# Attention loop in another order, and two unbinding products of the last block moved from GpSimd to VectorE

## What is computed

```python
def unit_projection(x):
    f = jnp.fft.fft(x)
    f = f / (jnp.abs(f) + EPS)
    return jnp.fft.ifft(f).real
...
        query = unit_projection(jnp.einsum('bsd,ed->bse', x, Wq) + bq)
        keys = unit_projection(jnp.einsum('bsd,ed->bse', x, Wk) + bk)
        values = unit_projection(jnp.einsum('bsd,ed->bse', x, Wv) + bv)
        x_k = bind(keys, values)          # ifft(fft(keys) * fft(values)).real
        s = jnp.cumsum(x_k, axis=1)
        out = unbind(s, query)            # ifft(fft(s) * conj(fft(query))).real
...
    h = _layernorm(x, axis=-1) * (1 + ca) + sa
    x = x + ga * _L0_attn_ref(h, ...)
    h = _layernorm(x, axis=-1) * (1 + cb) + sb
    x = x + gb * _L0_ffn_ref(h, ...)      # top 2 of 8 experts by h @ gate_w, softmax of the two, SwiGLU
```

## Time and profile before

| | |
|---|---|
| median of three runs | 638.22 us (636.01 to 638.6) |
| the profiled execution | 634.83 us |
| its span, first to last instruction | 633.0 us |
| TensorE busy | 565.5 us (89%) |
| VectorE busy | 490.1 us (77%) |
| ScalarE busy | 301.8 us (48%) |
| GpSimd busy | 322.2 us (51%) |
| mean granted TensorE clock | 0.935 |

### The profile page before, as it was taken

How to read it: one execution, slowest core, us unless ns; L and a number is a source line. 1 busy time by engine, 2 the same in 40 slices (tenths; PEclk the granted TensorE clock), 3 DMA queues, 4 the chain that set the end, 5 groups by cost and what they waited for, 6 DMA issues and landing times.

```text
span 633.0 us, 13199 instructions
## 1 busy us (share of the span) xinstructions
PE 565.5 (89%) x4005; PEld 428.1 (68%) x4006; DVE 490.1 (77%) x1058; ACT 301.8 (48%) x497; POOL 322.2 (51%) x213
## 2 busy tenths in 40 slices
PE   6888999899999966559699999999999999999982
PEld 5444554555546543326488888888888888888871
DVE  1238789989998988897378888888888888888881
ACT  3664877877786762532333333333333333333330
POOL 0002132441413243000638888888888888888554
PEclk9798999989997995857799999999999999999996
DMA  9213273652735328622747777777777777777632
GB/s 318 86 61 124 67 204 100 193 149 83 216 101 169 102 88 285 211 38 67 196 62 134 135 138 135 137 136 134 134 135 133 133 133 133 133 134 134 98 35 34
DMA packets 86942, 82.93 MB, mean 131 GB/s; under 512 B 48628, under 2 KB 76276, under 8 KB 86648
## 3 DMA queue, kind: packets, MB, share of 16 engines
q0 software_dynamic: 18480, 34.51, 30.3%
q1 hardware_dynamic: 67128, 47.07, 25.9%
q10 hardware_dynamic: 1296, 0.87, 0.4%
HBM read 45.90 MB, written 23.15 MB: 109 GB/s over the span
## 4 chain that ended last, share of the span: by engine, by line
PE 70%; DVE 12%; ACT 6%; issue 6%; DMA 3%; POOL 1%; POOLq 0%; SPq 0%; ACTq 0%; DVEq 0%
PE ps L703 33%; PE ps L720 16%; PE ps L484 9%; PE ps L540 3%; ACT region L801 2%; PE ps L494 2%; PE ps L636 1%; DMA w_stage<-in_w 1%; ACT region L857 1%; DVE region L1140 1%; DVE region L1180 1%; PE ps L425 1%; POOL region L1544 1%; PE ps L527 1%; DMA region<-in_dft 1%
## 5 line engine op out<-in xcount | busy, mean ns | idle before, releaser
L703 PE MATMUL ps<-region,w_sb 128*128 128x256 f16 x1872 | 213.4, 275 | 2.7 <-ACT region L939 2.7
L703 PEld LDWEIGHTS ps<-region,w_sb 128*128 x1872 | 184.2, 99 | 25.7 <-issue 3.0
L1574 POOL DMA_INDIRECT out_rows<-w_stage,region x78 | 150.5, 1930 | 48.5 <-DVE w_stage L1491 26.5
L1564 POOL DMA_INDIRECT region<-h_scratch,region x78 | 106.0, 1359 | 71.4 <-DVE region L1437 47.9
L1459 DVE TENSOR_SCALAR region<-ps,region 128x256 f32<-128x256 f32 x156 | 68.1, 478 | 61.0 <-PE ps L703 60.9
L720 PE MATMUL ps<-region 128*128 x936 | 110.2, 275 | 3.4 <-DVE region L1473 3.4
L720 PEld LDWEIGHTS ps<-region 128*128 128x128 f16 x936 | 92.3, 99 | 15.0 <-issue 3.6
L1015 ACT ACTIVATE region<-ps,region 128x256 f32<-128x256 f32 x156 | 65.5, 471 | 76.4 <-PE ps L703 76.4
L1025 ACT ACTIVATE region<-region 128x1024 f16<-128x1024 f32 x39 | 41.2, 1058 | 125.3 <-DVE region L1467 125.3
L484 PE MATMUL ps<-region 128*128 128x512 f32 x192 | 88.3, 617 | 8.4 <-ACT region L815 6.0
L1544 POOL TENSOR_TENSOR region<-region 128x512 f32<-128x512 f32 x32 | 39.7, 1267 | 94.3 <-DVE region L1167 94.3
(11 more groups left out here) (208 smaller groups left out, 683.8 us busy)
## 6 DMA issues: line engine op xcount, KB each, us to landing
w_stage<-in_w SPq DMA_DIRECT2D x20, 512.0 KB, 3.6
region<-in_x SPq DMA_DIRECT2D x8, 512.0 KB, 8.2
out_rows<-region SPq DMA_DIRECT2D x8, 512.0 KB, 3.0
h_scratch<-gb_bc SPq DMA_DIRECT2D x4, 1024.0 KB, 6.8
h_scratch<-region SPq DMA_DIRECT2D x8, 512.0 KB, 3.0
region<-region POOLq DMA_DIRECT2D x7, 512.0 KB, 4.6
region<-in_ramp SPq DMA_DIRECT2D x1, 2064.0 KB, 10.8
region<-in_w SPq DMA_DIRECT2D x4, 512.0 KB, 5.1
```

The source lines that it names most:

```text
L703: mm = pe.matmul(ps[:, GV + 2 * half + a, (f % 2) * MT:(f % 2 + 1) * MT], w, xg_t[:, s, xa * KD + k, :], start=(n == 0), stop=(n == 3 * KD ...
L1564: G.indirect_dma_start(out=xg_rows[:, t % XG, u, :], out_offset=None, in_=h_scratch, in_offset=bass.IndirectOffsetOnAxis(ap=gather_idx[:, ...
L1574: G.indirect_dma_start(out=out, out_offset=bass.IndirectOffsetOnAxis(ap=scatter_idx[:, at:at + 1], axis=0), in_=y_sb[:, t % 2, u, :], in_o ...
```

## The change

- TensorE: `project` is cut in three: the transposes (still `project`), `transform` (the six products) and `nyquist_cols`. In iterations 1 to 6 the first residue piece comes between the transform and the Nyquist columns, and the second one ahead of `nyquist_sums`. In iteration -1 it also transposes block 1 ahead of the pieces.
- ScalarE: in `evacuate` the first piece of the iteration is copied ahead of the last square, and the Nyquist columns behind it. `project` (the next standard deviation) and `std2` come ahead of the second piece, the gates behind it. `normal_rows` of block t + 2 comes ahead of the fourth piece and of the root of t + 1, where it stood behind both. In iteration -1 the root of block 0 comes after one weight split, and block 1's `spectra` ahead of the pieces; the splits of chunks 2 and 3 move into the evacuation of block 1.
- VectorE: `top2` reads the gates of block t - 3 instead of t - 2, and comes ahead of `nyquist_apply`; the one left over, of block 5, comes behind the loop. `ln1_rows` comes ahead of `unbind`. In block 0, `modulation` comes inside `bind`, behind `den`.
- Last block: GpSimd makes only the first two products (a = 0); VectorE makes the two others into `prod[:, IM]` itself, ahead of its sums.
- `low_weights` of ScalarE waits for `g_ready` instead of `x1_ready`; `roots` waits for the Nyquist columns.

```diff
@@ psum_plan
-            items += [("z", t + 1, i) for i in range(6)] + [("ny", t + 1, 0)]
+            items += [("z", t + 1, i) for i in range(6)]
+        if t == -1:
+            items += [("ny", 0, 0), ("lo", 0, 0)]
+        elif t < NBLK:
+            items.append(("lo", t + 1, 0))
+            if t + 1 < NBLK:
+                items.append(("ny", t + 1, 0))
+        if t < NBLK:
+            items.append(("lo", t + 1, 1))
         if 0 <= t < NBLK:
             items.append(("pre", t, 0))
-        if t < NBLK:
-            items.append(("lo", t + 1, 0))
         if t >= 2:
             items.append(("gate", t - 2, 0))
         if t < NBLK:
-            items += [("lo", t + 1, 1), ("lo", t + 1, 2)]
+            items.append(("lo", t + 1, 2))
@@ TensorE, the loop
             for t in range(-1, NBLK):
-                if t + 1 < NBLK:
-                    project(t + 1)
                 if t == -1:
+                    project(0)
+                    transform(0)
+                    nyquist_cols(0)
                     modulation_rows()
+                    project(1)
+                    low_piece(0, 0)
+                elif t + 1 < NBLK:
+                    if t >= 1:
+                        project(t + 1)
+                    transform(t + 1)
+                    low_piece(t + 1, 0)
+                    nyquist_cols(t + 1)
+                else:
+                    low_piece(t + 1, 0)
                 if t >= 2:
                     gate_rows(t - 2)
-                if 0 <= t < NBLK:
+                low_piece(t + 1, 1)
+                if t >= 0:
                     nyquist_sums(t)
-                low_piece(t + 1, 0)
                 if t >= 2:
                     gate(t - 2)
-                low_piece(t + 1, 1)
                 low_piece(t + 1, 2)
@@ ScalarE, evacuate
-                    if c == 2:
-                        act.wait_ge(nymm, t + 1)
-                        if t < 2:
-                            act.wait_ge(ny_zero, t + 1)
-                        cols = rot(("ny", t, 0))[:, 0:3 * TPB].rearrange("p (j c) -> p c j", j=TPB)
-                        nc.scalar.activation(mag[:, t % 2, :, BLK:NB], cols, ACT.Square)
-                        nc.scalar.activation(z[:, t % 2, :, RE, BLK:NB], cols, ACT.Copy).then_inc(ny_out, 1)
+                    if c == 2 and t == 1:
+                        split_weights(2)
+                        split_weights(3)
+                    if c == 2 and t >= 1:
+                        low_piece(t, 0)
                     act.wait_ge(z_ready, 6 * t + 2 * c + 2)
                     nc.scalar.activation(sq[:, c], z[:, t % 2, c, :, 0:BLK], ACT.Square).then_inc(sq_ready, 1)
                     if c == 0 and t >= 2:
                         residual(t - 2)
+                act.wait_ge(nymm, t + 1)
+                if t < 2:
+                    act.wait_ge(ny_zero, t + 1)
+                cols = rot(("ny", t, 0))[:, 0:3 * TPB].rearrange("p (j c) -> p c j", j=TPB)
+                nc.scalar.activation(mag[:, t % 2, :, BLK:NB], cols, ACT.Square).then_inc(ny_out, 1)
+                nc.scalar.activation(z[:, t % 2, :, RE, BLK:NB], cols, ACT.Copy).then_inc(ny_out, 1)
@@ ScalarE, the loop
                 if t == LAST:
                     residual(t - 1)
+                    low_piece(NBLK, 0)
+                if t == -1:
+                    split_weights(0)
+                    roots(0)
+                    split_weights(1)
+                    modulation_rows()
+                    spectra(1)
+                    low_piece(0, 0)
                 if t >= 2:
                     gate_rows(t - 2)
-                if t == -1:
-                    split_weights(0)
-                    split_weights(1)
-                    modulation_rows()
-                low_piece(t + 1, 0)
+                if t >= 0 and t + 2 < NBLK:
+                    project(t + 2)
+                if t >= 1:
+                    std2(t - 1)
+                low_piece(t + 1, 1)
                 if t >= 2:
                     gate(t - 2)
-                if t >= 1:
-                    std2(t - 1)
-                if t >= 0 and t + 2 < NBLK:
-                    project(t + 2)
-                low_piece(t + 1, 1)
                 low_piece(t + 1, 2)
                 if t >= 0:
                     nyquist_row(t)
+                if t >= 0 and t + 2 < NBLK:
+                    normal_rows(t + 2)
                 low_piece(t + 1, 3)
-                if t + 1 < NBLK:
+                if 0 <= t < NBLK - 1:
                     roots(t + 1)
                 if t >= 0 and t + 2 < NBLK:
-                    normal_rows(t + 2)
-                if t + 2 < NBLK:
                     spectra(t + 2)
@@ VectorE, bind
+                if t == 0:
+                    modulation()
                 dve.wait_ge(den_ready, t + 1)
@@ VectorE, unbind
-                dve.wait_ge(x1_ready, 2 * (t + 1))
+                if t == LAST:
+                    dve.wait_ge(scan_ready, 2 * (t + 1))
+                    for r in range(2):
+                        ins = V.tensor_tensor(prod[:, IM, r, 0:BLK], s_run[:, t % 2, IM, :], z[:, t % 2, QRY, r, 0:BLK],
+                                              ALU.mult)
+                    ins.then_inc(x1_own, 1)
+                    dve.wait_ge(x1_own, 1)
+                dve.wait_ge(x1_ready, 2 * t + (1 if t == LAST else 2))
@@ VectorE, the loop
+                if t >= 3:
+                    top2(t - 3)
                 if 0 <= t < NBLK:
                     nyquist_apply(t)
-                    if t >= 2:
-                        top2(t - 2)
+                    if t + 2 < NBLK:
+                        ln1_rows(t + 2)
                     unbind(t)
                     if t + 1 < NBLK:
                         magnitudes(t + 1)
                 if t == -1:
                     ln1_rows(1)
-                    modulation()
                     magnitudes(0)
-                if t >= 0 and t + 2 < NBLK:
-                    ln1_rows(t + 2)
...
+            top2(LAST - 2)
             early_picks()
@@ GpSimd
-                for a in range(2):
+                for a in range(1 if t == LAST else 2):
```

More of the change, by code:

```diff
@@ L477, in project, with transform @@
                 transpose_rows(n_sb, t, tp_done)
+            def transform(t):
                 for i in range(6):
@@ L486, in project, with nyquist_cols @@
                     mm.then_inc(z_mm, 1)
+            def nyquist_cols(t):
                 bank_free(pe, ("ny", t, 0))
@@ L897, in low_weights @@
             def low_weights(t):
-                act.wait_ge(x1_ready, 2 * NBLK)
+                act.wait_ge(g_ready, 2 * NBLK)
                 for i in range(4):
@@ L973, in _ @@
                     nyquist_row(t)
+                if t >= 0 and t + 2 < NBLK:
+                    normal_rows(t + 2)
                 low_piece(t + 1, 3)
-                if t + 1 < NBLK:
+                if 0 <= t < NBLK - 1:
                     roots(t + 1)
                 if t >= 0 and t + 2 < NBLK:
-                    normal_rows(t + 2)
-                if t + 2 < NBLK:
                     spectra(t + 2)
-                if 1 <= t <= NBLK:
+                if t >= 1:
                     split_rows(t - 1)
-                split_weights(2 * t + 4)
-                split_weights(2 * t + 5)
+                if t >= 0:
+                    split_weights(2 * t + 4)
+                    split_weights(2 * t + 5)
             last_residual(0)
```

5 lines of the change are left out of this document (3 added, 2 removed).

## The result

| | before | after |
|---|---|---|
| median of five runs | 638.22 us (636.01 to 639.33) | 633.25 us (633.15 to 636.28) |
| the profiled execution | 634.83 us | 633.15 us |
| its span | 633.0 us | 631.3 us |
| mean granted TensorE clock | 0.935 | 0.927 |

The ratio is 0.9929 (0.9903 to 0.9954): 5.0 us or 0.8% faster, where 9.0 were forecast.

What follows compares the result with a forecast made beforehand. VectorE was taken to set the period of the eight blocks ahead of the expert stage. 8.7 us to block 7 plus 1.1 in the last block, less 0.8 for the clock: 9.0 us, 638.22 to 629.2, range 625.3 to 634.5.

Steps and rivals of the forecast that it cites:

- The loop: Blocks 1 to 7: without VectorE's wait for the gates, periods of 25.4 us (odd) and 26.3 (even); block 7 at 223.3.
- signs of being wrong: Blocks 2 to 6: L1125 waiting for L504, L1132 for L850, or the clock under 0.9 in more than one.
- The start: Ahead of block 1: block 0 starts 7.1 us earlier, its third step 3.7, block 1 at 68.3, 2.3 us gained.
- 1.5 more: Small work on TensorE behind block 1's transform: at the lower clock, 1.5 us more of the start's gain goes.
- The last block: Block 7: GpSimd makes half the products, VectorE two in 1.3 us; unbinding at 18.3 instead of 19.35, 1.1 us gained.
- -1 if not: Last block: if TensorE is not warm, since it idles before the inverse, -1 us instead of a gain of 1.1.
- the 0.8 kept for the clock: Blocks' small Nyquist matmuls: half a clock fall allowed for, 0.8 us, at 1.8 us a block.
- All behind hangs on this point and moves with it: Everything behind the last block, the expert stage included, was taken to move earlier by the whole gain.
- The clock: Rival: TensorE's clock falls in three blocks, 5.4 us back, gain 4.5, 633.7 us; chance 0.20.
- The start giving nothing: Rival: block 1's root behind the normal rows with TensorE low takes the 2.3 us, 631.5 us; chance 0.12.
- The change not doing what it says: Rival: gates' wait becomes one on TensorE's sums or ScalarE's root every block, 1.5 us left, 636.7; chance 0.09.
- Slower: Rival: clock stays low from Nyquist columns through inverse, VectorE waits 4.1 us in six blocks, 653 us; chance 0.07.

Runs made afterwards that it cites:

- e11: The changed kernel with VectorE's maxima of the gates back in their old place, behind the Nyquist product; 633.64 us, 0.9992 of before.
- e7: The kernel before with only the maxima of the gates taken one block later, ahead of the Nyquist product; 638.24 us, 0.9989 of before.
- e5: The changed kernel with, at block 0 alone, Nyquist columns and sums ahead of the residue pieces; 630.66 us, 0.9874 of before.
- e12: The changed kernel with the start undone on ScalarE and VectorE; 634.51 us, 1.0014 of before.
- e3: The changed kernel with GpSimd making all four products of the last block again; 634.94 us, 0.9938 of before.
- e1: The kernel before, run and profiled again unchanged; 637.84 us, 0.9996 of before.
- e10: The kernel before with the first gathers issued by pairs of tiles, nothing of the change; 634.87 us, 1.0005 of before.
- e8: The changed kernel with gathers of tiles 2 and 3 waiting for the first up product, 4 and 5 for the second; 630.11 us, 0.9869 of before.
- e9: The changed kernel with block 0's Nyquist sums ahead of the residue pieces and gathers by pairs of tiles; 628.88 us, 0.9912 of before.
- e2: The changed kernel, run and profiled again unchanged; 634.1 us, 0.9934 of before.
- e4: The changed kernel with gathers of tiles 2 to 5 issued only after the first tile's up products; 634.64 us, 0.9957 of before.

## Why the forecast was right in its direction and 4 us off

**The loop: right.** Block 1 to block 7 took 154.87 us; the forecast had 155.0 (223.3 less 68.3; its own periods add up to 155.3, block 3's start being 0.3 too early in its list), from 161.45. Its steps are in the traces: the wait for the gates gone; GpSimd's products just in time and waited for in block 6 alone, 0.6 us; the sums of the unbinding 1.12 each in even blocks, hence 26.15 against 25.46; L1175 at 0.70. One of the forecast's signs of being wrong did show once, the wait of 1.8 us for TensorE's sums in block 6, without a longer block. Ten profiles of kernels with the changed loop give 154.9 to 155.1 us in six, 159.2 to 162.1 in four (one of these is e11, with the maxima undone). e7 adds what the forecast didn't claim: the late maxima alone bring nothing. What they bring in the new order e11 doesn't separate from the clock.

**The start: the term was mis-sized.** The forecast put block 1 at 68.3, a gain of 2.3; it came at 70.03, a gain of 0.6. Block 0's start (37.59, forecast 38.4) and its third step (42.01, forecast 43.0) were 0.8 and 1.0 better. What failed is the row of small work on TensorE behind the transform: priced at the full clock, with "1.5 more" if at the lower one. It was at the lower: the Nyquist columns took 2.83 us and the second piece's pair 2.05 (59.77), VectorE's unbinding began at 63.30 instead of 62.3, and the Nyquist row reached ScalarE at 65.60 instead of 63.6, so that root and block 1 were 1.7 late. The price was right and the wrong side was taken. e5 moves the sums out of that row and gets 1.8 to 2.6 us back. By e12 beside e11 the start is worth 1.3 us in the changed order, and that order itself uses 2.4, which is in no term of the forecast.

**The last block: wrong.** The products took 1.28 us as priced, without the overlap with GpSimd (its half ended at 241.75, they began at 241.73). The Trainium skill (GPSIMD Engine Reference, Specifications), by which the two engines contend where VectorE reads two inputs, is neither borne out nor refuted by this place, since they did not overlap. The unbinding came at 18.15 us, forecast 18.3. But 0.9 of the 1.2 us were lost by the last moments: on TensorE the second piece's pair (1.91 us, at the lower clock) stood ahead of the inverse, which began 1.76 us behind the unbinding instead of 1.29, and whose own first pair took 1.03 us instead of 0.59. Behind that, to the gather, 0.35 more went. Forecast 1.1, measured 0.0 to 0.2 (67.27 and 67.14 against 67.26; e3 67.35). The forecast had this case, "-1 if not" warm, and took the warm one, as at the start; the cold one cost less than its price.

**The sum at the gather.** 299.32 less 9.8 is 289.5; less the 0.8 kept for the clock, 290.3. Measured 292.17: 1.7 from the start, 1.1 from the last block, 0.1 better in the loop, and the 0.8 not needed.

**"All behind hangs on this point and moves with it": wrong in a way the trace of before could not show.** The first profile of before had 335.5 us behind the gather, that of after 341.0. The span came out at 631.3 instead of 624.0; of these 7.3 us 5.5 are the stall behind the gather, and 1.9 lie ahead of it. On the medians most of the 5.5 cancels, since before has the stall as well on the two chips where it was looked for (e1 340.6, e7 339.4), and its profiled execution without it lies 3.4 us under its median. That leaves 2.1 us of the 4.0 between 629.2 and 633.25; the other 1.9 are the start and the last block. Where the 2.1 us lie is open. Either a usual execution of before reaches the gather sooner than at 299.32, from which the 9.0 were counted: e1 does, at 295.69, but it is the fastest of its runs. Or the stall costs before less than the changed kernel: e7 reaches the gather at 299.75 and needs 1.6 us less behind it than after did. The two blocks at the low clock and 27.3 us were no sign of an odd execution: e10 has the same two (27.33 and 27.43 us at 0.88), and e1 has two others.

The measured 633.25 us lie inside the range, 625.3 to 634.5, near its upper end. The stall was none of the reasons given for the range, so that it held is in part luck.

**The rivals.** The clock: real and priced right where a low block follows another (1.4 to 2.1 us a block, forecast 1.8), but the first low block costs 0.4 at most (0.3 to 0.4 in e3, e8 and e9, nothing in block 6 of after and e5), and the number of blocks is not fixed; of the nine profiles with the late maxima three lose 4 to 7 us by it (e3, e8, e9), and the scatter of the changed kernels' runs comes with it (e3: 632.15 us at a mean clock of 0.932, 637.32 at 0.916, 640.13 at 0.909). The start giving nothing: nearly what happened, 0.6 of 2.3 us. The change not doing what it says: no. Slower, with VectorE 4.1 us late in six blocks: no; even with five blocks low, the loop of e8 took 162.11 us, 7 more than at its best, not 25. The rule of the Trainium skill quoted there (TensorE: Matmul & The Clock Gate, A second HAM failure mode) says that short idle times between groups of matmuls can make the level go up and down. The level does so within one loop here (0.93, 1.00, 0.93, 1.00, 0.93 and 0.87 in blocks 1 to 6 of after), but also between executions of one kernel (e2: 1.00 in five of the six blocks). No run varied the idle times alone, so that they are the reason isn't shown.

**Open.** Why TensorE and ScalarE stand while the gathers run: the experiments show that it follows the gathers and goes with fewer in a row, not through what; that TensorE's code comes in late behind them, the theory of e4, is neither shown nor excluded. Whether the stall goes with the chip or with the execution: the eight profiles of after and e1 to e7, with eight or twelve gathers in a row, have it; the first profile of before had none, and neither had the two on the last chip. Where 2.1 us of the forecast's error lie. What decides whether the clock falls in an execution. And the changed kernel's ratio on the chip without the stall, where e9, the changed kernel with two further edits, is ahead of before (0.9912) and e11 and e12, each with one part undone, are not.

## What to carry to other kernels

Before a gain is counted from one profiled execution, take its time beside the timed runs: if it lies outside them, as 634.83 did under 636.01 to 639.33, some part of it isn't the usual one. Which part it is, only further profiles of the same kernel tell: here it was the gathers, not the loop with its low-clock blocks. A wait that is taken away is worth what is late next: here the late maxima gave nothing alone. And small work behind a dense stretch is priced at the lower clock first, above all where somebody waits for it: the two terms that fell short, the start and the last block, had been priced at the full one.

## What the runs showed of the hardware

A burst of twelve indirect gathers by GpSimd (292.17 to 307 us, one each 1.26 us) went with a stall of TensorE and ScalarE in eight profiles: instructions that waited for nothing came 0.3 to 1.1 us apart, and the rest of the execution took 339.4 to 341.6 us instead of 334.4 to 335.5. With at most four in a row it didn't happen (337.2 to 337.5), and in two profiles on a third chip and in one of the kernel before it didn't happen with twelve. A VectorE step of two inputs (128x516) took 0.70 us alone; twice it fell under a GpSimd tensor operation of 2.1 us and then ended 0.55 us behind that operation's end, whether it had started 0.12 us behind its start (2.56 us) or 0.93 (1.76 us). A block of the changed loop took 25.45 to 26.33 us at a granted clock of 0.93 to 1.00; at 0.87 or 0.88 it took 0 to 0.4 us more if it was the first such block, and 1.4 to 2.1 more if another stood directly ahead of it.
